# The front of a batch (norm, projections, spread of Q and K) moved into the end of the preceding batch of its stream

## What is computed

```python
h = layernorm(x) * (1 + ca) + sa          # ca, sa, ga, ...: per batch and channel
# 16 heads of 8 channels, causal, over 512 tokens
q, k, v = h @ W_UQ, (h @ W_DKV) @ W_UK, (h @ W_DKV) @ W_UV
x = x + ga * (softmax(q k^T / sqrt(8), causal) @ v) @ W_O
h = layernorm(x) * (1 + cb) + sb
for l in range(2):                         # 8 heads of 64, window of 64 + 64 tokens
    qkv = shift_token(h) @ wqkv[l]
    q, k = rotary(l2norm(q) * qs, l2norm(k) * ks)
    h = h + local_attention(q, k, v) @ wo[l]
    g = layernorm(shift_token(h)) * lg + lb
    a, b = split(g @ w1[l] + b1[l])
    h = h + (a * gelu(b)) @ w2[l] + b2[l]
out = x + gb * h
```

## Time and profile before

| | |
|---|---|
| median of 3 runs | 2705.08 us (2704.16 to 2709.94) |
| the profiled execution | 2719.58 us |
| its span, first to last instruction | 2717.7 us |
| TensorE matmul busy | 2255.4 us, 83% of the span |
| VectorE busy | 1653.4 us, 61% |
| ScalarE busy | 1592.6 us, 59% |
| GpSimd busy | 558.3 us, 21% |
| mean granted TensorE clock | 0.943 |
| DMA | 78.60 MB, 14.2% of 16 engines by the queue of SyncE |

### The profile page before, as it was taken

The page is one execution under the profiler, slowest core; times in us unless marked ns, Lnnn a source line. Parts: engine busy times, 40 slices in busy tenths (PEclk is TensorE's granted clock), DMA queues, the critical chain, the costliest instruction groups (busy, mean ns, idle before and its releaser), DMA issues. The chain is left out here.

```text
span 2717.7 us, 51718 instructions
## 1 busy us (share of the span) xinstructions
PE 2255.4 (83%) x20546; PEld 1405.6 (52%) x20746; DVE 1653.4 (61%) x2633; ACT 1592.6 (59%) x3047; POOL 558.3 (21%) x512
## 2 busy tenths in 40 slices
PE   2589977999789897798977988779987899679997
PEld 2455644546556454555555554455644555445464
DVE  1466655676556665567665676656765666556765
ACT  1357654667457664577545776447754567546665
POOL 2012230231202420024200232002320121302311
PEclk9799988999899998899989999889999999899998
DMA  4200122001210002201022011210122001220010
GB/s 103 40 8 15 29 51 38 7 9 29 52 38 16 19 17 47 38 15 29 20 41 31 15 29 31 39 21 15 29 43 40 8 15 29 48 35 9 7 29 22
DMA packets 62519, 78.60 MB, mean 29 GB/s; under 512 B 9266, under 2 KB 57132, under 8 KB 59948
## 3 DMA queue, kind: packets, MB, share of 16 engines
q1 hardware_dynamic: 62284, 75.29, 14.2%
HBM read 11.37 MB, written 4.19 MB: 6 GB/s over the span
## 5 line engine op out<-in xcount | busy, mean ns | idle before, releaser
L858 DVE TENSOR_REDUCE nm<-ps 128x2 f32<-128x768 f32 (+3 forms) x384 | 387.6, 1043 | 304.4 <-PE ps L547 300.3
L989 POOL TENSOR_TENSOR pr<-pr 128x1024 f32<-128x1024 f32 x128 | 302.2, 2361 | 1057.8 <-DVE pr L895 1057.8
L786 ACT ACTIVATE pr<-ps,wb,inv 128x128 f32<-128x128 f32 x1024 | 368.5, 481 | 121.5 <-DVE wb L912 121.1
L546 PE MATMUL ps<-K,Q 128*128 128x128 bf16 x1024 | 209.2, 232 | 201.0 <-issue 175.6
L492 PE MATMUL ps<-cf,pr 128*128 128x128 f32 x2048 | 289.0, 281 | 74.9 <-POOL pr L999 61.2
L743 ACT ACTIVATE pr<-ps 128x896 f32<-128x896 f32 x256 | 233.2, 921 | 193.9 <-PE ps L565 192.9
L492 PEld LDWEIGHTS ps<-cf,pr 128*128 128x128 f32 x2048 | 226.8, 142 | 138.1 <-POOL pr L999 76.3
L888 DVE TENSOR_TENSOR pr<-ps,rot 128x1024 f32<-128x1024 f32 x128 | 156.5, 1223 | 155.9 <-ACT pr L758 153.4
L906 DVE TENSOR_REDUCE wm<-ps 128x8 f32<-128x1024 f32 x128 | 156.6, 1224 | 123.9 <-PE ps L642 122.0
L546 PEld LDWEIGHTS ps<-K,Q 128*128 128x128 bf16 x1024 | 105.6, 104 | 224.8 <-issue 191.5
L758 ACT ACTIVATE pr<-ps 128x1024 f32<-128x1024 f32 x128 | 131.1, 1024 | 135.1 <-PE ps L613 80.0
(11 more groups left out here) (142 smaller groups left out, 4468.4 us busy)
## 6 DMA issues: line engine op xcount, KB each, us to landing
pr<-V SPq DMA_DIRECT2D x32, 520.0 KB, 4.5
Q<-scr SPq DMA_DIRECT2D x224, 64.0 KB
K<-scr SPq DMA_DIRECT2D x224, 64.0 KB
pr<-V SPq DMA_DIRECT2D x32, 390.0 KB, 6.1
xn<-in_L_attn_x SPq DMA_DIRECT2D x16, 256.0 KB, 2.9
out<-hT SPq DMA_DIRECT2D x16, 256.0 KB, 2.2
Q<-in_c_edge SPq DMA_DIRECT2D x32, 64.0 KB
Q<-mT SPq DMA_DIRECT2D x128, 4.0 KB
```

The costliest lines, as they stand in the source:

```text
L546: pe.matmul(last_tile, lhs, K1[s][:, h, wd - P:wd], start=True, stop=False)
L786: ins = act.activation(P2[s][:, 2 * (p % 2) + r, o:o + P], bank[:, r * T + o:r * T + o + P], ACT.Exp, scale=inv[s][:, t, h:h + 1], bias=wb ...
L858: dve.tensor_reduce(nm[s][:, qt, h0:h0 + n], src, AX_X, ALU.max, negate=True).then_inc(nm_r[s], 1)
L989: pool.tensor_tensor(t1[s][t % 3], t1[s][t % 3], t2[s], ALU.add).then_inc(sum_r[s], 1)
```

## The change

Five things are done together.

1. The front of a batch stands in the order inside the last layer of the preceding batch of its stream: load behind pturn 3 of the last layer, center 0 behind wctx 3, spread 0 behind wturn 2, proj behind wturn 3. Behind these come wout, center 3, spread 3, hid, down and final of the preceding batch, and then the rest of the new batch.
2. So that both can live at the same time, the front writes other buffers: x goes to xT1 and the rests to a part of pr, y1, the square, the root and the six bf16 parts to K2, all of the same stream and free by then. The DMAs go into Q and K as before.
3. Two new steps stand behind final: keep, a GpSimd copy of 128x512 f32 from xT1 to xT, which waits for the preceding batch's final; and values, which is the matmul for v with its four ScalarE copies (and the two GpSimd memsets that were in load), taken out of proj. score 0 on ScalarE and out on VectorE wait for keep.
4. The small copy of the batch's six modulation values (cur, 128x6) goes; VectorE reads them out of mod.
5. ALL and FIRST_BANKS are new: another interleaving of the two streams, and another choice of banks. The semaphores of center and spread of n = 0 are separate ones.

No matmul, activation or DMA of the front is added or taken away beside the keep copy and the cur copy.

```diff
 def steps():
-    out = [("load",), ("center", 0), ("spread", 0), ("proj",)]
...
-    out += units[0] + [("rows1", 0)] + units[1] + [("rows1", 1)]
+    out = [("keep",), ("values",)] + units[0] + [("rows1", 0)] + units[1] + [("rows1", 1)]
...
-    return out + [("final",)]
+    out += [("final",)]
+    cut = out.index(("pturn", DEPTH - 1, NP2 - 1)) + 1
+    first = {("pturn", DEPTH - 1, NP2 - 1): ("load",), ("wctx", DEPTH - 1, NP2 - 1): ("center", 0),
+             ("wturn", DEPTH - 1, NP2 - 2): ("spread", 0), ("wturn", DEPTH - 1, NP2 - 1): ("proj",)}
+    between = [(0, first[out[cut - 1]])]
+    for name in out[cut:]:
+        between += [(1, name)] + [(0, first[name]) for _ in range(name in first)]
+    return between + [(0, name) for name in out[:cut]]
...
-        parts = [[a[:, i * 256:(i + 1) * 256].bitcast(BF16) for i in range(6)] for a in scr]
-        rest = [[a[:, 1536 + i * T:1536 + (i + 1) * T] for i in range(2)] for a in scr]
+        early = [a[:, :, :].rearrange("p a n -> p (a n)") for a in K2]
+        parts = [[a[:, i * 256:(i + 1) * 256].bitcast(BF16) for i in range(6)] for a in early]
+        y1 = [a[:, 3 * T:4 * T] for a in early]
+        sq1 = [a[:, 0:T] for a in early]
+        rs1 = [a[:, T:2 * T] for a in early]
+        rest = [[a[:, i * T:(i + 1) * T] for i in range(2)] for a in flat]
+        xT1 = [a[:, 2 * T:3 * T] for a in flat]
...
                     if kind == "load":
-                        if b >= S2:
-                            banks.wait(act, (b - S2, "final"))
-                        act.activation(xT[s][:, :], banks.wait(act, (b, "xT")), ACT.Copy).then_inc(xt_r[s], 1)
+                        act.activation(xT1[s], banks.wait(act, (b, "xT")), ACT.Copy).then_inc(xt_r[s], 1)
...
+                        if h == 0:
+                            act.wait_ge(*keep_r.at(b, 1))
...
-                    if kind == "load":
+                    if kind == "keep":
+                        pool.wait_ge(*xt_r.at(b, 1))
+                        if b >= S2:
+                            banks.wait(pool, (b - S2, "final"))
+                        pool.tensor_copy(xT[s][:, :], xT1[s]).then_inc(keep_r[s], 1)
+                    elif kind == "values":
```

More of the change, by code:

```diff
@@ L100, in merged @@
         for bit in range(3, -1, -1):
-            b, group = next(rest[int(digit, 16) >> bit & 1], (0, []))
-            out += [(b, name) for name in group]
+            group = next(rest[int(digit, 16) >> bit & 1], [])
+            out += [(b, name) for b, name in group if 0 <= b < B]
     assert len(out) == B * len(names)
@@ L107 @@
 ORDER = merged()
[L110 to L135, removed]
@@ L509, in step @@
                             pe.wait_ge(*hsp_r.at(b, 2 * (n - 2) + 2))
-                        bank, full = banks.take(pe, (b, "xc", n), [sq_r.at(b, n + 1)])
-                        pe.matmul(bank, centre, (xT if n < 2 else hs)[s][:, :], start=True, stop=True).then_inc(full, 1)
+                        bank, full = banks.take(pe, (b, "xc", n), [sq_r[n].at(b, max(n, 1))])
+                        src = xT1[s] if n == 0 else (xT if n == 1 else hs)[s][:, :]
+                        pe.matmul(bank, centre, src, start=True, stop=True).then_inc(full, 1)
                     elif kind == "spread":
                         n, = a
-                        bank, full = banks.take(pe, (b, "var", n), [rs_r.at(b, 2 * n + 1)])
-                        pe.wait_ge(*sq_r.at(b, n + 1))
-                        pe.matmul(bank, mean, sq[s], start=True, stop=True).then_inc(full, 1)
+                        bank, full = banks.take(pe, (b, "var", n), [rs_r[n].at(b, 2 * max(n, 1) - 1)])
+                        pe.wait_ge(*sq_r[n].at(b, max(n, 1)))
+                        pe.matmul(bank, mean, (sq if n else sq1)[s], start=True, stop=True).then_inc(full, 1)
                     elif kind == "proj":
@@ L718, in step @@
                         bank = banks.wait(act, (b, "xc", n))
[L719 to L720 removed]
+                        act.activation(y[s][:, :] if n else y1[s], bank, ACT.Copy).then_inc(xc_r[n][s], 1)
+                        act.activation((sq if n else sq1)[s], bank, ACT.Square).then_inc(sq_r[n][s], 1)
                     elif kind == "spread":
                         n, = a
[L723 to L725 removed]
+                        dst = (rs if n else rs1)[s]
+                        act.activation(dst, banks.wait(act, (b, "var", n)), ACT.Ln, bias=eps[:, 0:1]).then_inc(rs_r[n][s], 1)
+                        act.wait_ge(*rs_r[n].at(b, 2 * max(n, 1) - 1))
+                        act.activation(dst, dst, ACT.Exp, scale=-0.5).then_inc(rs_r[n][s], 1)
                     elif kind == "proj":
```

87 lines of the change are left out of this document (56 added, 31 removed).

## The result

| | before | after |
|---|---|---|
| median, of 4 runs each | 2707.51 us (2704.16 to 2714.65) | 2464.77 us (2462.40 to 2467.29) |
| ratio after / before | | 0.910 (95%: 0.9078 to 0.9123) |
| profiled execution / its span | 2719.58 / 2717.7 us | 2463.41 / 2461.6 us |
| mean granted clock | 0.943 | 0.979 |

The change takes 243 us off the median. The prediction had 177 us less (2528 us), and its range, 2478 to 2605, lies wholly above the result.

The account below looks back on a forecast made before the run. TensorE was taken to bound the kernel, with gaps while max 0 waits for spreads; 175.6 + 31 - 7 - 16 - 7 = 176.6 us less than 2705.1 gave 2528 us, range 2478 to 2605.

Parts of the forecast that it names:

- 1, 3: gaps before max 0: TensorE's waits before max 0: 15 gaps, 175.6 us in all, go, 7 us left in even batches, 7 in batch 1.
- 4: row copies at score 8: Score 8 waits for row copies queued behind the spreads: 4 us in each of batches 3, 5, 9 and 11, 16 us.
- 2: clock: TensorE's work at 1.2 GHz in and behind the gaps runs at 2.4 GHz: 2.1 us a gap, 31 us saved.
- 5, 6: all small waits: The front's own waits, and those around GpSimd and VectorE, keep their price: 0 for each of the two terms.
- need: From proj's first matmul through the spreads' landing to max 0: 28.0 us in an even batch, 30.5 in an odd one.
- cover: TensorE's work between proj and max 0; in the new order 29.5 us in even batches, more than enough in odd ones.
- step 6: GpSimd and VectorE beside the moved fronts: 0, ends -30 (half of today's heads' wait for GpSimd) and +35.
- Better than the sum: Rival: no gap stays, the clock stays up, heads stop waiting for GpSimd (+30): 2469 us, chance 0.13.
- VectorE becomes the bound beside the max steps: Rival: max 0 to 11 beside wscore to wturn overload VectorE, 40 us lost: 2596 us; chance 0.24 for VectorE or rows.
- The rule on two SBUF inputs: GpSimd and VectorE contend for SBUF in VectorE's moved product of two SBUF operands: up to 20 us, taken as 0.
- slower rival: The gap moves to score 8 or max 0 again and the front's waits come on top: 2783 us, chance 0.04.

Follow-up runs that it names:

- e12: The changed kernel itself, run once more on the same chip as e9; measured 2463.5 us.
- e4: The changed kernel with proj of the even batches 2 to 14 put behind down of the preceding batch; measured 2644.4 us, ratio to before 0.975.
- e9: The changed kernel with group 2's row copies issued between Q's 14 spreads and K's 14 of the other stream's odd batches; 2437.9 us, 0.901 of the kernel before.
- e7: The kernel before with only the fronts moved, other steps in the old order, each result keeping its old bank; 2685.3 us, ratio 0.991.
- e8: The changed kernel's order and banks, but each front bare between final and max 0 of its stream; 2966.0 us, a single run.
- e2: The kernel before with each PSUM bank chosen as the one used longest ago; measured 2836.3 us, ratio 1.048.
- e1: The changed kernel with each PSUM bank (or pair) chosen as the one used longest ago; measured 2627.1 us, ratio to before 0.970.

## Why the prediction was wrong, by its steps

The sum was 176.6 us. Between the like traces (before and e12) it is 255.6, of which some 12 us are the profiled execution of before being slower than its median. Term by term:

| step | predicted | measured |
|---|---|---|
| 1, 3: gaps before max 0, with what is left in even batches and batch 1 | -161.6 | -171.3 (175.6 to 4.3) |
| 4: row copies at score 8 | +16 | +19.9 (8.3 of them in batch 1) |
| 2: clock, TensorE's busy time | -31 | -57.7 |
| 5, 6: all small waits | 0 | about -47 |
| start, batch 0 | 0 | about +1 |

**Steps 1, 3 and 4 held.** Need and cover are the right account. The need was 28.0 and 30.5 us; e4 has 26.1 from the first command against 26.3, e12 has 29.3 against 28.8. The 7 us that I had left in even batches came to 4.3, in three of them. The 7 us left in batch 1 came at score 8 and not at max 0: 8.3 us in e12, 0.6 in the first trace of the changed kernel. In batches 3, 5, 9 and 11 the row copies cost 9.6 us in e12 and 16 in the first trace, against 16, and in batch 7, where I had counted on hid, 2.0 and 1.3. That they can't count as landed before the spreads' data on the same DMA engines was the rule of the Trainium skill (DMA: Bandwidth & Descriptors, Queues, rings and completion order). e12 agrees: 10.2 us from the issue to the matmul that waits, where 2 to 3 had been the other choice; in the earlier trace rows the spreads of batch 7 took about as long, 9.8 us from the last issue to max 0. And e9, which puts them ahead of half the spreads, ends the wait.

**Steps 5 and 6 failed.** "They keep their price in a new place: 0" and "Both unmeasured: 0" were the terms that were mis-sized, by some 47 us. I had priced the waits as belonging to the front's steps. What the traces show is that waits of many other steps changed with their neighbours and their banks. L516, the wait of the four norms, went from 30.3 to 19.2 us (17.7 + 1.5). The row turns (L554, now L569) went from 16.4 to 8.7 for VectorE, with 5.3 us for ScalarE that are new, and the heads' wait for GpSimd from 61.2 to 52.5: that last one fell as step 6 thought possible (-30 was its lower end), by less. The remaining one to name is wscore (L633 is its first matmul). In the kernel before, TensorE waited there 18.9 us, in three lines:

```profile
PE ps L633 <- ACT Kf L775: 12.3, 18, 1.2
...
PE ps L633 <- DVE scr L846: 5.4, 7, 1.2
...
PE ps L633 <- ACT pr L786: 1.2, 3, 0.4
```

It now waits 2.0 us in e12 for other engines. For the last layer of the odd batches, where most of the 12.3 us were, the order says why: wscore 0 followed the last heads step at once, and now two max steps of the other stream stand between them. The 5.4 us were a wait for a bank that VectorE's part of proj still read, and proj no longer stands there. Such distances and banks are what the new order was free to choose. It is not shown which of them gave how much. What is shown: the same move in the old order with the old banks adds 98 us of small waits, 70 of them for banks (e7), and the new order without the move leaves them where they were, 192 against 190 (e8).

**Step 2 failed in kind, not only in size.** "15 gaps, 2.1 us each" counted the work at 1.2 GHz behind the gaps alone. Summed over windows of 2 us through the whole span (busy time, times twice what the clock lacks of 1.0), the kernel before did 144 us of TensorE's busy time at half clock, of which the 15 gaps explain some 63 (15 x 4.2, and as much when the windows behind all 15 are summed). The rest stood elsewhere, much of it in thin stretches without a long gap. In e12 it is 54 us, in the first trace of the changed kernel 72. Half of the difference, 45 us (36 by the first trace), is time saved by the clock, an estimate. The remaining 13 us of the 57.7 are not explained. In e7, where the gaps went and thin stretches came, it is still 138.

**A reading.** The prediction sees "a 7, 8 or 9 in a third of the slices" of the clock line; all 40 are that, and 11 are a 7 or an 8. Nothing rests on it.

**The rivals.** "Better than the sum" (2469 us, 0.13) has the right time by luck, not the right way to it: GpSimd gave 9 us of its 30, the rest came from waits that it did not name and from the clock. "VectorE becomes the bound beside the max steps" is wrong: the wait of the row turns for VectorE halved, and the period is 291 us with 204 of VectorE. The rule on two SBUF inputs (the Trainium skill, GPSIMD Engine Reference, Key points) cost nothing here: the moved product took 691 to 693 ns in all 16 batches, as the trace of the changed kernel says.

```profile
L846 DVE TENSOR_TENSOR Kf<-Kf x16: 691/693/693, 48.5 to 2151.4; 128x512 f32<-128x512 f32 x16
```

The slower rival's time did not come, though its mechanism is real in a small form: a wait did move to score 8, and it is the 20 us that e9 takes back. What I hadn't thought of is that the move could do almost nothing for want of a fitting order and fitting banks. I took both as given and priced only the part that the move needs of them, when most of the gain hangs on all three.

**Open.** How much of the merge's part is distance between dependent steps and how much a better pairing of engines; whether a better order for the old fronts would have closed part of the gaps (e8 is not such an order); what the banks of the change are worth against the best ones for the old order; and what the move alone would give with banks made for e7's order, the nearest rival to the reading that the order decides.

## What to carry to other kernels

Price a wait that a transfer causes by need (issue to landing) and cover (work between), and check every other user of the queue it is issued on: here two small copies moved ahead of 14 others were worth 1% more. When a change moves steps in an order that is written out, the small waits and the clock are terms of their own, of both signs: the same move gave 24 us in the old order with the old banks, 79 where a rule picks the banks in both kernels, and 243 with an order and banks made for it. When a wait names a line whose result the waiting instruction doesn't read, look for a shared bank. Compare busy times only between traces with about the same number of records.

## What was not expected of the hardware

- The granted clock falls in stretches that are only thin. In e7 it is 0.55, 0.50 and 0.84 over 15 us in which TensorE is busy for 2.94, 3.84 and 3.09 of each 5 us, after a window at 1.00 in which it was busy for 2.26 of 5; no single wait there is over 2.9 us.
- A choice of PSUM banks that fits the order is worth 135 us of 2701 (e2) and 162 of 2465 (e1) here, with not one instruction more or less.
- The row copies of 4 KB each, issued behind 28 copies of 64 KB, were there 10.2 us after their issue (e12, batch 7).
